# Order of TensorE's work in a half key block of attention: both scores first, then the two products of the maxima

## What is computed

```
Q, K, V = layernorm(x) @ W.T + b, in 16 heads of 16
A   = softmax(Q K^T / 4)                       per head, 2048 x 2048
out = (0.6 * A + 0.4 * L) @ V                  L: a band of 7 keys around each query
x   = x + out @ Wo.T + bo
x   = x + mixture of 4 experts, 2 per token (layernorm(x))
```

## Time and profile before

| | us |
|---|---|
| median of 3 runs (lowest, highest) | 1991.12 (1990.95, 1991.9) |
| span of the profiled execution | 2006.8 |
| TensorE busy, matmuls, in the span | 1951.3 |
| VectorE busy | 1626.5 |
| ScalarE busy | 1374.2 |
| granted TensorE clock, mean | 0.995 |

### The profile page before, as it was taken

How to read it: one execution, slowest core, us unless ns; L and a number is a source line. 1 busy time by engine, 2 the same in 40 slices (tenths; PEclk the granted TensorE clock), 3 DMA queues, 4 the chain that set the end, 5 groups by cost and what they waited for, 6 DMA issues and landing times. The chain is left out here.

```text
span 2006.8 us, 47862 instructions
## 1 busy us (share of the span) xinstructions
PE 1951.3 (97%) x16384; PEld 1036.7 (52%) x16384; DVE 1626.5 (81%) x2075; ACT 1374.2 (68%) x2471; POOL 346.9 (17%) x379
## 2 busy tenths in 40 slices
PE   7999999999999999999999999999998799999997
PEld 3543333333333333333333333333687689999997
DVE  6799999999999999999999999994255565555564
ACT  3358888888888888888888888889544422233332
POOL 1361010001000100001000100010024532232233
PEclk9999999999999999999999999999999899999999
DMA  7954355335643454336534554341123677788884
GB/s 266 245 111 92 78 102 115 74 74 97 108 90 74 90 99 106 74 80 102 113 74 74 100 105 90 74 93 54 42 74 131 242 235 227 245 269 297 263 272 113
DMA packets 105849, 264.09 MB, mean 132 GB/s; under 512 B 20896, under 2 KB 52768, under 8 KB 99104
## 3 DMA queue, kind: packets, MB, share of 16 engines
q1 hardware_dynamic: 92624, 245.29, 48.6%
q0 software_dynamic: 13152, 17.83, 4.6%
HBM read 206.95 MB, written 73.94 MB: 140 GB/s over the span
## 5 line engine op out<-in xcount | busy, mean ns | idle before, releaser
L626 DVE TENSOR_REDUCE part_max<-psum 128x1 f32<-128x1024 f32 x1024 | 1240.8, 1222 | 50.6 <-PE psum L750 37.7
L681 ACT ACTIVATE probs<-psum 128x512 f32<-128x512 f32 x2048 | 1111.1, 596 | 145.4 <-PE psum L763 78.2
L763 PE MATMUL psum<-score_q,score_k 50*128 50x512 f32 x2048 | 745.9, 446 | 0.1
L750 PE MATMUL psum<-max_k,max_q 48*128 48x512 f32 x2048 | 737.9, 449 | 0.5 <-DVE part_max L626 0.4
L775 PE MATMUL psum<-probs,v_ones 128*32 128x256 f32 x8192 | 654.1, 391 | 9.4 <-ACT heads_sb L696 9.0
L763 PEld LDWEIGHTS psum<-score_q,score_k 50*128 50x128 f32 x2048 | 306.9, 184 | 404.7 <-ACT probs L681 390.7
L775 PEld LDWEIGHTS psum<-probs,v_ones 128*32 128x32 f32 x8192 | 162.1, 107 | 380.8 <-issue 198.1
L750 PEld LDWEIGHTS psum<-max_k,max_q 48*128 48x128 f32 x2048 | 294.2, 185 | 12.8 <-issue 7.0
L1184 ACT ACTIVATE x_sb<-psum,x_sb 128x512 f32<-128x512 f32 (+1 forms) x160 | 101.6, 636 | 257.8 <-PE psum L1564 243.1
L1583 PE MATMUL psum<-w,h_hi 128*128 128x256 f32 x1120 | 202.1, 279 | 2.7 <-DVE h_lo L1385 2.5
L1583 PEld LDWEIGHTS psum<-w,h_hi 128*128 128x128 f32 x1120 | 178.7, 189 | 13.8 <-DVE h_lo L1385 3.2
(11 more groups left out here) (185 smaller groups left out, 1352.3 us busy)
## 6 DMA issues: line engine op xcount, KB each, us to landing
w<-w_split SPq DMA_DIRECT2D x40, 2048.0 KB, 7.9
max_q<-qk_pieces SPq DMA_DIRECT2D x192, 128.0 KB, 7.2
score_k<-qk_pieces SPq DMA_DIRECT2D x192, 128.0 KB, 4.7
xs<-in_pads SPq DMA_DIRECT2D x33, 528.0 KB, 8.3
qk_pieces<-pieces SPq DMA_DIRECT2D x32, 512.0 KB, 4.6
w_split<-w_pair SPq DMA_DIRECT2D x32, 512.0 KB, 8.8
max_k<-qk_pieces SPq DMA_DIRECT2D x192, 64.0 KB, 8.2
score_q<-qk_pieces SPq DMA_DIRECT2D x192, 64.0 KB, 2.2
```

What stands on the lines that cost most here:

```text
L626: nc.vector.tensor_reduce(part_max[:, t, p:p + 1], ps_m[p].rearrange("q b f -> q (b f)"), axis=AXIS.X, op=ALU.max).then_inc(m_read, 1)
L681: nc.scalar.activation(probs[kb % 2][:, chunk * BLOCK:(chunk + 1) * BLOCK], bank_of(at), ACT.Exp, scale=float(HD) ** -0.5).then_inc(exp_do ...
L750: last = nc.tensor.matmul(ps_m[p][:, h, :], max_q[u][rows, t * P:(t + 1) * P], max_k[u][rows, p * BLOCK:(p + 1) * BLOCK], start=True, stop ...
L763: nc.tensor.matmul(bank_of(at), score_k[u][rows, kb * P:(kb + 1) * P], score_q[u][rows, part * BLOCK:(part + 1) * BLOCK], start=True, stop ...
```

## The change

In each half block TensorE gets both scores first, then the two products of the maxima, then the values. The waits are the same ones and stand with their instructions. In terms of row tiles the four matmuls ahead of the values went to 0, 1, 0, 1 and now go to 0, 1, 1, 0.

```diff
@@ -842,17 +842,17 @@
                     if more_scores:
                         scores(*nxt, 0, ends)
+                    if more_scores:
+                        scores(*nxt, 1, ends)
                     if more_maxima:
                         maxima(g, ahead % ST, mu, 0)
-                    if more_scores:
-                        scores(*nxt, 1, ends)
                     values(n, kb, u, 0, ends)
                     if more_scores:
                         scores(*nxt, 2, ends)
+                    if more_scores:
+                        scores(*nxt, 3, ends)
                     if more_maxima:
                         maxima(g, ahead % ST, mu, 1)
-                    if more_scores:
-                        scores(*nxt, 3, ends)
                     values(n, kb, u, 1, ends)
```

## The result

The changed kernel takes 1997.07 us (median of 8 runs, 1996.36 to 1998.59) against 1991.53 us (8 runs, 1990.95 to 1992.48): 5.5 us more, a ratio of 1.0029 with a 95% interval of 1.0019 to 1.0039, which is 3.8 to 7.8 us. The forecast was slower, 2001.2 us, in a range of 1994 to 2009.

What follows compares the result with a forecast made beforehand. TensorE's own chain was taken to bound the kernel. Steady half blocks +2.9, waits after the transpose of the maxima +6.9 and after the heads' transposes +0.3 made +10.1 us on 1991.1: 2001.2 us, range 1994 to 2009.

Steps and rivals of the forecast that it cites:

- The bound: In half blocks with maxima, TensorE alone sets the pace by its own chain, 1.24 us each; VectorE could take 1.13.
- The held score: After the transpose of the maxima, both maxima queue behind the waiting second score: 0.89 against 0.66 us, 30 times, +6.9 us.
- upper bound: After the transpose of the maxima: 0.28 us each if the exponential's release came 0.05 later, +8.4 us.
- lower bound: After the transpose of the maxima: 0.11 us each if row tile 0 went on alone, +3.3 us.
- The steady half block: Row tile order 0, 1, 1, 0 delays the fourth load behind the third: 0.003 us in each of 982, +2.9 us.
- The half block after the heads' transposes: Second half block after them: second score waits 0 to 0.02 us for an exponential, 0.01 taken, 30 times, +0.3 us.
- The margin: Steady half block: second score's bank is free before its load is wanted; margin falls from 0.17 to 0.06 us, cost 0.
- rival 2: Second score late in every half block, a stall of 0.02 us each, about 2021 us; chance 0.10.
- rival 1: Second pair in each half block: pairs of one kind run faster, 0.01 us each, 1988.5 us; chance 0.11.
- rival 3: Third load no longer overlaps the matmul on its own row tile: +0.09 us per half block, about 2086 us; chance 0.03.
- rival 4: New stall is absorbed, by VectorE setting the pace or the second exponential ending earlier: 1991.1 us; chance 0.06.

Runs made afterwards that it cites:

- e1: Changed kernel with the old order restored only in the half block after the transpose of the maxima; 1992.96 us, ratio 1.0009.
- e2: Kernel before with the new order only in the half block after the transpose of the maxima; 1998.11 us, ratio 1.0032.
- e7: Changed kernel with a ring of two PSUM banks for the scores instead of three; 2221.3 us, ratio 1.1159.
- e9: Kernel before with the second score moved between the two matmuls of the maxima, row tiles 0, 1, 1, 0; 1991.15 us, ratio 0.9999.
- e4: Kernel before with the two matmuls of the maxima swapped, row tiles 0, 0, 1, 1; 1993.1 us, ratio 1.0008.

## Why the prediction was right, and where it was off

**The bound** was read rightly. TensorE's own chain sets 1.24 us; VectorE's six reductions take 7.42 us before and after, and each delay on TensorE came out in the time.

**The held score** was the right mechanism in the right place: 0.89 us forecast for the half block, 0.88 found; 6.9 us forecast, 6.6 found, shown by e1 and e2, which take that one half block out and put it in alone, and by e7, where the held score comes in over half of all half blocks and the two orders stand 114 us apart. The upper bound of the step was not needed. Its lower bound, that row tile 0 goes on alone, is half true: it goes on alone as soon as the load is released (e9), but that is no gain where two matmuls of row tile 1 come one after the other.

**The steady half block** is the step that failed, and it is a term of the sum that was mis-sized: +2.9 us forecast, +0.1 found in the means by place (and in e1 all of what is left in the stretch is 0.8 us). The text said that the third load goes to the tile loaded second and that the fourth must queue behind it. e4 shows that it needn't: each row tile takes its next work itself, the load for row tile 0 goes first although it stands last, and the pair of loads comes after the same 0.11 us.

**The half block after the heads' transposes:** +0.3 forecast; the means by place have 0.006 us there, 0.2 us in all, but no more than some other places differ by.

**The margin** of 0.06 us for the second score's wait held (rival 2 is out: the load never lags in a steady half block). **Pairs of one kind** are not faster (rival 1: 0.34 us from pair to pair as before). **The third load** overlaps the matmul that runs on its own row tile (rival 3): maxima load 0.11 us after the scores, whose matmuls take 0.50. The rule of the Trainium skill named there, that a weight load overlaps only matmuls of another row group, does not hold in this trace. **Nothing to be seen** (rival 4) is out by the interval.

The sum was +10.1 us, the result +5.5 (3.8 to 7.8), at the lower end of the range forecast. Without the mis-sized term the sum would have been +7.2. That term's size, 0.003 us a half block, was a choice inside a rounding of 0.01 us times 982, which no row could have told from zero.

## What to carry to other kernels

A wait that costs nothing may do so only because it stands last: when an instruction with a wait is moved forward, look up how long it is held now, even where nobody idles for it, and count what comes to stand behind it on the same part of the engine. Such a place shows in a timeline as a load that starts late in its group (0.22 us instead of 0.11), not in a list of idle times. And read the places where the pattern is broken, once per head here, before the steady part: they carried all of this change.

## What the runs showed of the hardware that was not expected

The two row tiles of TensorE take work past each other: with the queue 0, 0, 1, 1 the third matmul starts beside the first, and the half block stays at 1.24 us (e4, 720.30 to 721.54). A held load, however, stops both (e9: the load of the other row tile goes at 0.22 us with the held one).

The signal of completion keeps the order of the queue all the same. In the changed kernel's half block after the transpose, the maxima's matmul of row tile 0 carries the signal and starts first. Alone it is there as

```profile
284.47 0.48 PE L750 MATMUL psum<-max_k,max_q 48*128 48x512 f32 x1
```

and would be done at 284.95; both are done at 284.47 + 0.61 = 285.08, and VectorE, idle for 0.41 us by then, starts its reduction at 285.13. One place would be little to build on, but there are more where the signalling matmul starts early and VectorE stands idle. In the changed kernel there are 32: the reduction starts 0.044 to 0.046 us after the modelled end of the later matmul, and 0.12 to 0.19 us after that of the signalling one. In e7 there are 692: 0.045 to 0.048 us, and 0.10 to 0.29. The ends are modelled, but a delay that is constant to 0.003 us from one of the two and not from the other shows which one VectorE waits for. This agrees with the part of the Trainium skill's rule ("TensorE: Matmul & The Clock Gate", "Part 3: Packing small matmuls") that says the last-issued matmul's signal covers the ones before it.
